# Expert stage of a two-layer transformer kernel: second-product parts ahead of the gate on TensorE, Newton step on GpSimd, output step behind the next expert's split

## The reference

```python
# gate, scaling and sum of the second layer's attention
x = x + ga * (proj.sum(axis=1) / H)                 # "project", then the row factor ga and the sum
h = _layernorm(x) * (1 + cb) + sb                   # first normalization
x_attn = (_layernorm(h) * ln_g + ln_b) @ attn_w + attn_b + h   # second normalization, "gate" product
g = x_attn.reshape(MICRO_BATCHES, E, tpe, D)        # 8 experts, 2 x 256 tokens each
a = gelu(g @ w1[e] + b1[e])                         # 256 -> 1024, "first"
y = a @ w2[e] + b2[e]                               # 1024 -> 256, "second"
out = gelu(y @ next_w + next_b)                     # "last"
x = x + gb * out                                    # "finish"
```

## Time and profile before

| | |
|---|---|
| median of three runs | 2117.03 us |
| the profiled execution | 2122.24 us, of it the span 2120.5 us |
| expert stage in the profile | about 1757 to 2117 us |
| busy in the whole span | PE 1865.6 us (88%), DVE 1351.8 us (64%), ACT 1209.5 us (57%), POOL 576.9 us (27%) |
| one steady cycle of the expert stage | 38.9 or 40.6 us |
| busy in such a cycle | PE 33.3 to 36.3 us, DVE 28.6 to 29.3 us, ACT 22.6 to 23.7 us, POOL 16.4 to 17.3 us |

### The profile page before, as it was taken

The page is one execution under the profiler, slowest core; times in us unless marked ns, Lnnn a source line. Parts: engine busy times, 40 slices in busy tenths (PEclk is TensorE's granted clock), DMA queues, the critical chain, the costliest instruction groups (busy, mean ns, idle before and its releaser), DMA issues. The chain is left out here.

```text
span 2120.5 us, 29755 instructions
## 1 busy us (share of the span) xinstructions
PE 1865.6 (88%) x10573; PEld 766.2 (36%) x10573; DVE 1351.8 (64%) x2591; ACT 1209.5 (57%) x1686; POOL 576.9 (27%) x668
## 2 busy tenths in 40 slices
PE   5789999988879999899899987899999883888887
PEld 3323323322234444444444432223333222444443
DVE  5478888888743553553544525888887754776771
ACT  4277778776742432333333324888888773564563
POOL 5666676671210000000001012111111001344443
PEclk8589999999999999999999997999999996999998
DMA  3344553344260000000000031233333305233210
GB/s 111 60 94 115 121 135 109 102 109 95 93 231 28 21 21 1 21 21 1 22 31 16 21 51 53 48 70 71 67 64 58 54 11 195 90 112 135 72 40 20
DMA packets 111988, 147.95 MB, mean 70 GB/s; under 512 B 11874, under 2 KB 95188, under 8 KB 109780
## 3 DMA queue, kind: packets, MB, share of 16 engines
q1 hardware_dynamic: 111828, 145.77, 25.9%
HBM read 100.34 MB, written 45.14 MB: 69 GB/s over the span
## 5 line engine op out<-in xcount | busy, mean ns | idle before, releaser
L824 DVE TENSOR_REDUCE A_M<-A_SM 128x1 f16<-128x512 f32 x1024 | 654.2, 686 | 179.8 <-PE A_SM L1033 177.8
L584 ACT ACTIVATE A_P<-A_ST 128x1024 f32<-128x1024 f32 x512 | 523.5, 1025 | 133.6 <-PE A_ST L1049 131.0
L1033 PE MATMUL A_SM<-A_KT,A_QS 48*128 48x512 f16 x1024 | 352.0, 399 | 62.0 <-DVE A_M L824 54.7
L1576 PE MATMUL B_PA<-B_Hh,B_wh 128*128 128x512 f16 x1024 | 388.1, 379 | 0.0
L1576 PE MATMUL B_PA<-B_Hl,B_wh 128*128 128x512 f16 x1024 | 388.1, 379 | 0.0
L1495 ACT ACTIVATE B_af<-B_PA,B_sv 128x512 f32<-128x512 f32 x192 | 131.9, 687 | 356.0 <-PE B_PA L1576 355.2
L1049 PE MATMUL A_ST<-A_QS,A_KT 49*128 49x512 f16 x1024 | 301.4, 387 | 0.2
L1066 PE MATMUL A_AV<-A_P,A_V 128*32 128x512 f32 x2048 | 280.9, 612 | 5.3 <-ACT A_P L584 4.8
L1033 PEld LDWEIGHTS A_SM<-A_KT,A_QS 48*128 48x128 f16 x1024 | 82.2, 94 | 441.4 <-DVE A_M L824 385.2
L1539 DVE TENSOR_SCALAR B_Hh<-B_af 128x512 f16<-128x512 f32 x128 | 58.4, 456 | 281.8 <-ACT B_af L1495 281.8
L1290 POOL TENSOR_TENSOR B_hl<-B_hf,B_hh 128x512 f16<-128x512 f32 x14 | 16.2, 1156 | 523.5 <-ACT B_hh L1306 523.5
(11 more groups left out here) (338 smaller groups left out, 3291.7 us busy)
## 6 DMA issues: line engine op xcount, KB each, us to landing
D_w_st<-in_we_dram SPq DMA_DIRECT2D x16, 1024.0 KB, 4.9
qk<-A_tr SPq DMA_DIRECT2D x58, 256.0 KB, 2.4
A_KT<-qk SPq DMA_DIRECT2D x96, 128.0 KB, 4.9
A_QS<-qk SPq DMA_DIRECT2D x96, 128.0 KB, 5.3
A_w_st<-in_w_ffn_dram SPq DMA_DIRECT2D x32, 352.0 KB, 3.6
w_hi<-A_f_hi SPq DMA_DIRECT2D x32, 176.0 KB, 3.5
w_lo<-A_f_lo SPq DMA_DIRECT2D x32, 176.0 KB, 3.8
B_wl<-w_lo SPq DMA_DIRECT2D x1, 5632.0 KB, 23.1
```

Source lines behind the costliest of these rows:

```text
L584: nc.scalar.activation(P[:, st, 2 * pair:2 * pair + 2, :], ST[:, u % 2, :, :], ACT.Exp, scale=1.0 / math.sqrt(HD)).then_inc(exp_s, 1)
L824: nc.vector.tensor_reduce(M[G % 2][:, tt, o:o + 1], SM[:, n % 2, :], AX, ALU.max, negate=True).then_inc(max_s, 1)
L1033: nc.tensor.matmul(SM[:, n % 2, :], QS[b % 2][r, 2 * g + pair, tt * 128:tt * 128 + 128], KT[b % 2][r, 2 * g + pair, :], start=True, stop=T ...
L1576: ins = nc.tensor.matmul(out, a, c, start=start and kt == 0 and n_ == 0, stop=stop and kt == kts[-1] and n_ == len(ops) - 1)
```

## The change

There are three edits, all inside `experts`.

1. TensorE: in each body the gate product moves from behind part 0 of the second product to behind part 1, and the two projections from behind parts 1 and 2 to behind parts 2 and 3.
2. The Newton step moves from DVE to POOL, where it is four small operations behind `pow` instead of three. DVE does the first pass over ht before it waits for the root, and waits for the second root directly before xn.
3. POOL does `prepare(b+2)` before `finish(m)`.

```diff
             def root_of(nth):
 
+                k = 4 * nth
                 pool.wait_ge(ve_s, nth + 1)
-                if nth >= 1:
-                    pool.wait_ge(newton, 3 * nth)
                 nc.gpsimd.tensor_tensor(r0[:, :], ve[:, :], power[:, :], ALU.pow).then_inc(guess, 1)
+                pool.wait_ge(guess, nth + 1)
+                nc.gpsimd.tensor_tensor(rt[:, :], r0[:, :], r0[:, :], ALU.mult).then_inc(newton, 1)
+                pool.wait_ge(newton, k + 1)
+                nc.gpsimd.tensor_tensor(rt[:, :], rt[:, :], ve[:, :], ALU.mult).then_inc(newton, 1)
+                pool.wait_ge(newton, k + 2)
+                nc.gpsimd.tensor_scalar(rt[:, :], rt[:, :], -0.5, 1.5, ALU.mult, ALU.add).then_inc(newton, 1)
+                pool.wait_ge(newton, k + 3)
+                nc.gpsimd.tensor_tensor(rstd[:, :], rt[:, :], r0[:, :], ALU.mult).then_inc(newton, 1)
...
                 if e is not None:
                     root_of(2 * e + 1)
+                if b + 2 < E8:
+                    prepare(b + 2)
                 if m is not None:
                     finish(m)
-                if b + 2 < E8:
-                    prepare(b + 2)
...
                 nc.vector.tensor_scalar(ve[:, :], mv[:, :, 1], EPS, None, ALU.add).then_inc(ve_s, 1)
-                dve.wait_ge(guess, nth + 1)
-                nc.vector.tensor_tensor(rt[:, :], r0[:, :], r0[:, :], ALU.mult).then_inc(newton, 1)
-                dve.wait_ge(newton, 3 * nth + 1)
-                nc.vector.scalar_tensor_tensor(out=rt[:, :], in0=rt[:, :], scalar=-0.5, in1=ve[:, :],
-                                               op0=ALU.mult, op1=ALU.mult).then_inc(newton, 1)
-                dve.wait_ge(newton, 3 * nth + 2)
-                nc.vector.scalar_tensor_tensor(out=rstd[:, :], in0=rt[:, :], scalar=1.5, in1=r0[:, :],
-                                               op0=ALU.add, op1=ALU.mult).then_inc(newton, 1)
-                dve.wait_ge(newton, 3 * nth + 3)
...
+                    dve.wait_ge(newton, 4 * (2 * e) + 4)
                     for tt in range(TT):
                         dve.wait_ge(u_s, TT * e + tt + 1)
...
+                    dve.wait_ge(newton, 4 * (2 * e + 1) + 4)
                     for tt in range(TT):
                         nc.vector.tensor_scalar(xn[:, tt, :], ht[:, tt, :], mv[:, tt, 0:1], rstd[:, tt:tt + 1],
...
-                    if a is not None and c == 0:
+                    if a is not None and c == 1:
                         gate(a)
-                    if e is not None and c in (1, 2):
-                        project(e, c - 1)
+                    if e is not None and c in (2, 3):
+                        project(e, c - 2)
```

## The result

| | kernel before | changed kernel |
|---|---|---|
| median | 2116.94 us (2116.18 to 2120.49, 4 runs) | 2137.11 us (2133.67 to 2141.53, 4 runs) |
| ratio, 95% interval | | 1.0086 (1.0067 to 1.0106) |
| profiled execution, span | 2120.5 us | 2139.8 us |
| gate to gate, five full cycles | 38.9 to 40.6 us, 199.5 in sum | 44.34 to 44.37 us, 221.8 in sum |

The changed kernel is 0.9% slower, about 20 us. The forecast was 2133.4 us and 0.8%. The five full cycles grew by 22.3 us and the one before them by 4.1 us. The body before that shrank by 1.3 us (31.13 against 32.43; 31.87 in a later profile of the same kernel), and the stretch behind the last gate by 5.1 us (47.0 against 52.1), while the stage itself began 0.6 us sooner. Together that is 19.4 us, and the spans differ by 19.3.

What follows compares the result with a forecast made beforehand. DVE was taken to set the expert cycle's second half, with TensorE having little slack. Five full cycles +16.8, the cycle before +3.0, the body before that +1.0 and the end -4.4 gave +16.4 on 2117.0: 2133.4 us, range 2120 to 2146.

Steps and rivals of the forecast that it cites:

- The kind of loss: Expert cycle: y2l comes later, TensorE becomes the bound with 18.7 us from y2l's end to the next gate.
- The test that I had named for it: DVE would stay the bound if y2l came less than 1.5 us later behind S than before.
- S: End of the second sum x3 + x2t, counted from the gate's start; forecast 15.3 us (14.7 to 15.8).
- the slack of 1.5 us: From y2l's end to the next gate: TensorE's 18.7 us against 20.25 us before, set by DVE.
- S to y2l: Time from S through the first root to y2l's end on POOL; forecast 7.05 us (6.4 to 7.7).
- The clock: TensorE at half clock behind a wait of some 8 us ahead of `last`; 2.2 us lost per cycle (1.7 to 2.8).
- The sum: Full expert cycle: 15.3 + 7.05 + 18.7 + 2.2 = 43.25 us (41.5 to 45.0).
- The first body: Body before the cycle from 1829.97: more TensorE work ahead of the gate, forecast +1.0 us (-1 to +2).
- The tail: Stretch from the last gate on: faster gate and two parts behind it instead of three, forecast -4.4 us.
- VectorE stays the bound: Rival for the expert cycles: DVE's savings on the second root and xn count in full; 2090 us, chance 0.06.
- The clock holds: Rival: TensorE comes out of the 8 us wait ahead of `last` at 2.4 GHz; 2120 us, chance 0.08.
- Much slower: Rival: every operation takes turns and half clock costs the full 2.8 us each cycle; 2146 us, chance 0.14.

Runs made afterwards that it cites:

- the filling: Changed kernel with thirty extra matmuls (tile 2's product five times ahead of its turn) in each of seven bodies, before `last`; 1.0006 to the kernel before.
- the early y2l: Changed kernel with y2l's two operations on GpSimd moved ahead of the sum x3 + x2t; 0.9865 to the kernel before.
- one wait more: The version with y2l moved ahead, where `finish` also waits for xn in the one body with an expert but no `prepare`; 0.9829, median 2089.69 us.
- the TensorE edit alone: Kernel before with only the gate product and the two projections each moved behind a later part of the second product; 0.9989.
- the root edit alone: Kernel before with only the Newton step moved to GpSimd, POOL's and TensorE's order as before; 1.0021.
- four buffers: Changed kernel with four x3 buffers in place of three, and el's wait on x4_s one expert later; 1.0042 to the kernel before.

## Why the prediction was right

**The kind of loss: right.** y2l became the bound through TensorE and not through VectorE. Between its end and the next gate TensorE had 18.7 us of work. Measured at full clock it is 18.5 (22.83 less the 4.3 us that the filling removed). The test that I had named for it was too crude, though. y2l moved by 1.5 us behind S (4.74 to 6.27), no more than the slack of 1.5 us, and with 18.5 us of work the slack was 1.7. That slack was counted against a VectorE that the change leaves alone. From S to xn's end VectorE took 14.2 us where it had taken 18.5, so TensorE would have been the bound with y2l unmoved: 4.7 + 18.5 = 23.2 us from S to the gate, against VectorE's 25.0 less 4.3.

**S: right.** 15.3 was forecast, 15.26 measured. el started 7.8 us behind the gate (7.5 to 7.9 forecast), released by `finish`, and took turns with gl.

**S to y2l: too long, and below its own range.** The term was 7.05 (6.4 to 7.7), and it measured 6.27. The step that failed is the worst case in which every small POOL operation takes turns with the first pass over ht. The pass took 1.66 us, as it did alone. pow took 1.18 in place of 1.02 us and the root 2.40 us in all, so these operations hardly cost each other anything. y2l and the second pass did take turns, but it was VectorE that paid. The pass took 3.43 in place of 1.67 us, and y2l lost only 0.18 us where I gave it 0.4. The Trainium skill's rule ("SBUF — State Buffer", "SBUF: two separate sides") agrees with this trace for the second pass beside y2l. For the small operations the price was far below the whole instruction that I had put in, and 7.7, which I had drawn from the rule, did not come.

**The clock: mis-sized.** 2.2 us per cycle was forecast with 2.8 as the top, and it was 4.3. I had taken the length of half clock from a stretch of 5.6 us. Behind the wait of 7.17 us it lasted for 9.5 us of work, all of `last` and half of tiles 2 to 4.

**The sum came out by two errors of opposite sign.** A full cycle was forecast at 43.25 and took 44.36: -0.04 in S, -0.8 in y2l, -0.2 in TensorE's work, +2.1 in the clock. That the sum lands within 1.1 us is in part luck. The first body gained 1.3 us where +1.0 was forecast. TensorE waits 3.37 us for ht there in place of 4.17, and my 1 us of added work does not show. In the second profile of the same kernel the gain is only 0.6 us, so half of it is scatter. The tail gained 5.1 against 4.4. Over the stage the signs cancel further, and 2137.1 lies 3.7 us from 2133.4.

**The rivals.** "VectorE stays the bound" fell: TensorE no longer waited for h2l or xn. "The clock holds" fell too, and the filling shows what it would have given: 1.0006, no change, as that rival's 2120 us said. The remark of the Trainium skill's "Perfetto Trace Analysis" ("Optimizing Scalar/DVE Operations"), that moving work between VectorE and GpSimd might not help, fits the Newton step by its size: 0.2% slower alone, 0.2 us a cycle gained with the early y2l. The loss alone isn't shown to come from a port; what the trace shows there is a late y2l and the half clock behind it. "Much slower" had one part right and one wrong: the clock cost more than its 2.8 us, the turns less.

## What to carry to other kernels

Before moving work into one wait, look at what it leaves uncovered at the next one: here 2.6 us of cover moved from a 1.7 us wait to a 2.8 us wait, and the smaller wait became the larger. When a chain goes through an engine that works strictly in its order, ask of each item in its queue who waits longest behind it; moving two short subtractions ahead of the sums and a root turned a loss of 0.9% into a gain of 1.3%, and with one wait more 1.7%. A grown wait on TensorE's path is to be priced with the half clock behind it, here 4.3 us behind a wait of 7.2; whether gathering the waits pays depends on it, and with the TensorE edit alone (one wait of 4.28 us) the time stayed the same.

## What the runs showed of the hardware that was not expected

- Half clock lasted much longer behind a wait than the wait itself: 9.5 us of work without a pause behind 7.17 us. Behind the same wait of 3.24 us (the root edit alone) it lasted for 3.4 or about 10 us, and the cycle was 39.6 or 42.5 us, in turn. Behind a wait of 1.69 us (the kernel before) it lasted for 3.4 us in three of six cycles and did not come in the others.
- In the changed kernel the full cycles have one length, 44.34 to 44.38 us in ten cycles of two executions. That is no rule: with four buffers and waits of 5.96 or 5.97 us they ranged from 40.65 to 43.49 us.
- Two operations that take turns don't pay alike, and it isn't always the same engine that pays. VectorE's second pass paid 1.8 us beside y2l and y2l 0.2 us; xn paid 3.8 us beside `finish`, and `finish` next to nothing. Beside the long el (1.1 us each) GpSimd paid too: gl took 3.25 in place of 2.3 us. Against VectorE's row of Hl, el and h2l without a gap (the kernel with the one wait more) it paid nearly everything: 6.32 us for one operation of 1.27 us, while VectorE lost nothing.
